# Attention by row pairs: bias rows added from their rows, K copied by ScalarE, the mask shared by two engines

## What is computed

```python
qkv = jnp.einsum('oc,bchw->bohw', qkv_w, x) + qkv_b[None, :, None, None]
q, k, v = (qkv[:, :C], qkv[:, C:2 * C], qkv[:, 2 * C:])
q = q * scale
k_u = unfold(k).reshape(B, nh, hd, L, ws * ws).transpose(0, 1, 3, 2, 4)
v_u = unfold(v).reshape(B, nh, hd, L, ws * ws).transpose(0, 1, 3, 4, 2)
k_g = k_u[:, :, attn_idx]
v_g = v_u[:, :, attn_idx]
attn = jnp.einsum('bnld,bnldk->bnlk', qh, k_g)
attn = attn + bias[None]
out = jnp.einsum('bnlk,bnlkd->bnld', attn, v_g)
```

## Time and profile before

| | us |
|---|---|
| median of 3 runs | 7908.27 (7907.89 to 7908.82) |
| profiled execution, its own time | 7900.45 |
| its span in the trace | 7898.5 |
| VectorE busy in the whole span | 6360.5 (81%) |
| TensorE, ScalarE, GpSimd busy | 6817.7 (86%), 5763.4 (73%), 5363.4 (68%) |
| row pairs of the first image, first to last add | 113.52 to 305.86 |
| row pairs of the second image, first to last add | 588.64 to 779.67 |

### The profile page before, as it was taken

One profiled execution on the slowest core, in us unless ns is written; L12 is line 12 of the kernel. 1 busy time (PEld: TensorE's weight loads), 2 busy tenths in 40 slices (PEclk: granted clock), 3 DMA queues, 4 the chain that ended last, 5 costly groups with the idle time before them and its releaser, 6 DMA issues. The chain is left out here.

```text
span 7898.5 us, 145982 instructions
## 1 busy us (share of the span) xinstructions
PE 6817.7 (86%) x42656; PEld 4640.5 (59%) x42656; DVE 6360.5 (81%) x9577; ACT 5763.4 (73%) x9016; POOL 5363.4 (68%) x3394
## 2 busy tenths in 40 slices
PE   5676787989968999999999999999999999999998
PEld 4444545767745666666666666665666666666666
DVE  3324184444439999999999999999999999999997
ACT  3416102222218999999999999999999999999997
POOL 3306000000009999999999999999999999999997
PEclk7878799999989999999999999999999999999998
DMA  1001000000010000000000000000000000000000
GB/s 65 22 3 38 0 0 0 0 0 0 0 58 10 1 1 1 1 1 1 10 1 1 1 1 1 1 27 1 1 1 1 1 2 2 3 3 3 4 4 5
DMA packets 75922, 55.73 MB, mean 7 GB/s; under 512 B 50776, under 2 KB 73464, under 8 KB 75032
## 3 DMA queue, kind: packets, MB, share of 16 engines
q1 hardware_dynamic: 72512, 53.88, 2.4%
q10 hardware_dynamic: 3288, 0.33, 0.0%
HBM read 37.80 MB, written 16.37 MB: 7 GB/s over the span
## 5 line engine op out<-in xcount | busy, mean ns | idle before, releaser
L1438 POOL TENSOR_TENSOR a_s<-a_s,a_v 128x784 f32<-128x784 f32 x1568 | 2910.3, 1856 | 429.5 <-ACT a_s L1650 414.0
L1474 PE MATMUL a_right_sides<-a_s,diag_d 128*128 128x392 f32 x6272 | 2281.7, 507 | 1.0 <-POOL a_s L1438 1.0
L1474 PEld LDWEIGHTS a_right_sides<-a_s,diag_d 128*128 128x128 f32 x6272 | 1130.6, 190 | 1035.9 <-issue 212.4
L1570 DVE SCALAR_TENSOR_TENSOR a_kan<-a_s,spline_c,a_kan 128x784 f32<-128x784 f32 x1568 | 1622.7, 1035 | 81.7
L1497 PEld LDWEIGHTS a_weighed<-a_V,a_probT 112*128 112x128 f32 x10976 | 1375.6, 193 | 162.2
L1431 POOL TENSOR_TENSOR a_inner<-a_inner,a_x 128x784 f32<-128x784 f32 x784 | 1456.8, 1858 | 0.0
L1497 PE MATMUL a_weighed<-a_V,a_probT 112*128 112x65 f32 x10976 | 1366.3, 270 | 0.0
L1650 ACT ACTIVATE a_s<-a_v 128x784 f32<-128x784 f32 x1568 | 1335.2, 852 | 4.6
L1641 ACT ACTIVATE a_v<-a_a 128x784 f32<-128x784 f32 x1568 | 1335.8, 852 | 0.3
L1486 PE MATMUL a_turned<-ident,a_prob 128*112 128x128 f32 x5488 | 856.7, 278 | 312.0 <-ACT a_probT L1657 305.7
L1461 PE MATMUL a_scores<-a_K,a_q 32*64 32x392 f32 x6272 | 699.6, 515 | 245.3 <-DVE a_kan L1552 214.6
(11 more groups left out here) (181 smaller groups left out, 6866.5 us busy)
## 6 DMA issues: line engine op xcount, KB each, us to landing
rows<-bias_rows_dram SPq DMA_DIRECT2D x112, 91.0 KB
X<-in_x_dram SPq DMA_DIRECT2D x4, 1568.0 KB, 15.8
a_q<-q_dram SPq DMA_DIRECT2D x392, 16.0 KB, 2.0
mask<-in_window_mask_dram SPq DMA_DIRECT2D x56, 98.0 KB
v_dram<-V SPq DMA_DIRECT2D x14, 227.5 KB, 2.3
a_V<-v_dram SPq DMA_DIRECT2D x4, 796.2 KB, 9.3
q_dram<-Q SPq DMA_DIRECT2D x14, 224.0 KB, 1.9
k_dram<-K SPq DMA_DIRECT2D x14, 224.0 KB, 1.9
```

The lines of the kernel that those rows point to most:

```text
L1438: eng.tensor_tensor(s, s, v, ALU.mult).then_inc(cubed, 1)
L1474: mm = eng.matmul(up[:, j, 0:SUB], steps[i][:, :], cubes[g][:, SUB * j:SUB * (j + 1)], start=(i == 0), stop=(i == 1))
L1570: eng.scalar_tensor_tensor(F, banked((s1, s2)[j][g][:, :]), c[:, 3 + j:4 + j], F, ALU.mult, ALU.add).then_inc(left_added, 1)
```

## The change

- The bias tile and ScalarE's copies into it are gone. VectorE adds the bias rows to the scores directly, with 8 instructions of 196 elements (L586 of the changed kernel) and 8 of 24 (L591); each reads one head of the rows, 8 floats apart, repeated over x.
- K's bias is added by ScalarE (L513), K and V have PSUM banks of their own (`kp[r]`, and `vp`, which exists once), and the scores wait for K's copy only; the weighing waits for V's.
- The mask is split: GpSimd multiplies 6 of the 8 blocks (L528), VectorE the other 2 (L597), right behind its add.
- SyncE loads the rows as soon as the add two tiles earlier is done, and the mask after both masks of two tiles earlier; the two kinds have semaphores of their own.
- The cleared margins are in `A` now, not in the bias tile.

```diff
             def _(sp):
                 def load(eng, t, r, turn):
-                    eng.wait_ge(masked, t + 1)
-                    eng.dma_start(mask[r][:, :], mask_dram[bass.ds(t, 1)].rearrange("t p c -> p (t c)")).then_inc(tables_loaded[r], 16)
-                    eng.wait_ge(bias_ready, t + 1)
+                    eng.wait_ge(scores_added, t + 1)
                     for q in range(2):
-                        eng.dma_start(rows[r][q * IMG:(q + 1) * IMG, :], bias_dram[bass.ds(2 * t + GRID * q, IMG), :]).then_inc(tables_loaded[r], 16)
+                        eng.dma_start(rows[r][q * IMG:(q + 1) * IMG, :], bias_dram[bass.ds(2 * t + GRID * q, IMG), :]).then_inc(rows_loaded[r], 16)
+                    eng.wait_ge(masked_p, t + 1)
+                    eng.wait_ge(masked_d, t + 1)
+                    eng.dma_start(mask[r][:, :], mask_dram[bass.ds(t, 1)].rearrange("t p c -> p (t c)")).then_inc(mask_loaded[r], 16)
...
             def _(act):
                 def stage(eng, t, r, turn):
-                    eng.wait_ge(kv_made, t + 1)
+                    eng.wait_ge(v_made, t + 1)
                     eng.activation(xt[r][:, :, :], xn[:, :, bass.ds(TILE * t, TILE)], ACT.Copy).then_inc(xt_ready, 1)
-                    eng.wait_ge(tables_loaded[r], 48 * (turn + 1))
+                    eng.wait_ge(k_made, t + 2)
                     eng.wait_ge(scores_added, t + 1)
...
                     for f in range(HALVES):
...
+                        eng.activation(kt[r][:, f, :], kp[r][:, f * TILE:(f + 1) * TILE], ACT.Identity, bias=m.qkvb[:, 2 + f:3 + f]).then_inc(kt_ready, 1)
+                act.sem_inc(kt_ready, 2 * HALVES)
                 ramp(act, stage, nothing)
...
                 def apply_mask(eng, t, r, turn):
-                    eng.wait_ge(tables_loaded[r], 48 * (turn + 1))
+                    eng.wait_ge(mask_loaded[r], 16 * (turn + 1))
                     eng.wait_ge(scores_added, t + 3)
-                    a = A[r][:, :, :, :].rearrange("p h f c -> p (h f) c")
-                    eng.tensor_tensor(a, a, mask[r][:, :].unsqueeze(1).to_broadcast([TILE, 8, COLS]), ALU.mult).then_inc(masked, 1)
...
+                    a = A[r][:, :, :, :].rearrange("p h f c -> p (h f) c")[:, 0:BY_POOL, :]
+                    eng.tensor_tensor(a, a, mask[r][:, :].unsqueeze(1).to_broadcast([TILE, BY_POOL, COLS]), ALU.mult).then_inc(masked_p, 1)
...
             def _(pe):
                 def front(eng, t, r, turn):
                     eng.wait_ge(xt_ready, t + 1)
-                    eng.wait_ge(kv_ready, 3 * (t + 1))
+                    eng.wait_ge(kt_ready, HALVES * (t + 1))
...
+                    mm.then_inc(k_made, 1)
+                    eng.wait_ge(vt_ready, t + 2)
                     for i in range(HALVES):
...
+                        mm = eng.matmul(vp[:, :], xt[r][:, i, :], m.WT[:, W_QKV + 8 + i:W_QKV + 12:2, :], start=(i == 0), stop=(i == HALVES - 1))
+                    mm.then_inc(v_made, 1)
+                    eng.wait_ge(kt_ready, HALVES * (t + 3))
                     eng.wait_ge(qt_ready, HALVES * (t + 1))
                     eng.wait_ge(scores_added, t + 2)
...
                 def back(eng, t, r, turn):
-                    eng.wait_ge(masked, t + 3)
+                    eng.wait_ge(vt_ready, t + 3)
+                    eng.wait_ge(masked_d, t + 3)
+                    eng.wait_ge(masked_p, t + 3)
                     eng.wait_ge(o_added, HALVES * (t + 1))
...
             def _(dve):
                 def front(eng, t, r, turn):
-                    eng.wait_ge(kv_made, t + 3)
+                    eng.wait_ge(v_made, t + 3)
+                    eng.tensor_tensor(vt[r][:, :], vp[:, :], m.vbias[0:TILE, :], ALU.add).then_inc(vt_ready, 1)
+                    eng.wait_ge(scores_made, t + 1)
+                    eng.wait_ge(rows_loaded[r], 32 * (turn + 1))
+                    window = rows[r][:, 0:WS * WIN * HEADS0].rearrange("p (y w e) -> p y w e", y=WS, w=WIN)
+                    beside = rows[r][:, WS * WIN * HEADS0:].rearrange("p (w s e) -> p w s e", w=WIN, e=HEADS0)
                     for f in range(HALVES):
-                        eng.tensor_scalar(kt[r][:, f, :], kvp[r][:, f * TILE:(f + 1) * TILE], m.qkvb[:, 2 + f:3 + f], None, ALU.add).then_inc(kv_ready, 1)
-                    eng.tensor_tensor(vt[r][:, :], kvp[r][0:TILE, 2 * TILE:2 * TILE + 2 * P], m.vbias[0:TILE, :], ALU.add).then_inc(kv_ready, 1)
-                    eng.wait_ge(scores_made, t + 1)
-                    eng.wait_ge(bias_ready, t + 3)
-                    eng.tensor_tensor(A[r][:, :, :, :].rearrange("p h f c -> p h (f c)"), scp[0:TILE, :, 0:HALVES * COLS],
-                                      bias[r][:, :, :, :].rearrange("p h f c -> p h (f c)"), ALU.add).then_inc(scores_added, 1)
+                        for h in range(4):
+                            cells = lambda ap: ap.rearrange("p (y x w) -> p y x w", y=WS, x=WS)
+                            eng.tensor_tensor(cells(A[r][:, h, f, 0:WS * WS * WIN]), cells(scp[0:TILE, h, f * COLS:f * COLS + WS * WS * WIN]),
+                                              window[:, :, :, 4 * f + h].unsqueeze(2).to_broadcast([TILE, WS, WS, WIN]), ALU.add)
+                    for f in range(HALVES):
+                        for h in range(4):
+                            cells = lambda ap: ap.rearrange("p (x w) -> p x w", w=WIN)[:, 1:WS, :]
+                            last = eng.tensor_tensor(cells(A[r][:, h, f, WS * WS * WIN:]), cells(scp[0:TILE, h, f * COLS + WS * WS * WIN:(f + 1) * COLS]),
+                                                     beside[:, :, :, 4 * f + h].rearrange("p w s -> p s w"), ALU.add)
+                    last.then_inc(scores_added, 1)
+                    eng.wait_ge(mask_loaded[r], 16 * (turn + 1))
+                    eng.wait_ge(scores_added, t + 3)
+                    a = A[r][:, :, :, :].rearrange("p h f c -> p (h f) c")[:, BY_POOL:8, :]
+                    eng.tensor_tensor(a, a, mask[r][:, :].unsqueeze(1).to_broadcast([TILE, 8 - BY_POOL, COLS]), ALU.mult).then_inc(masked_d, 1)
```

More of the change, by code:

```diff
@@ L456, in row_pairs0 @@
         mask = [sb(f"mask{r}", [TILE, COLS]) for r in range(2)]
-        bias = [sb(f"bias{r}", [TILE, 4, HALVES, COLS]) for r in range(2)]
         A = [sb(f"A{r}", [TILE, 4, HALVES, COLS]) for r in range(2)]
-        kvp = [ps(f"kvp{r}", [P, 512]) for r in range(2)]
+        kp = [ps(f"kp{r}", [P, 512]) for r in range(2)]
+        vp = ps("vp", [TILE, HALVES * P])
         scp = ps("scp", [P, 4, 512])
         op = ps("op", [P, 512])
[L464 to L467, removed]
+        xt_ready, qt_ready, k_made, v_made, kt_ready, vt_ready, margin_zeroed, scores_made, scores_added, o_made, o_added = (
+            sem(n) for n in ("xt_ready", "qt_ready", "k_made", "v_made", "kt_ready", "vt_ready", "margin_zeroed", "scores_made",
+                             "scores_added", "o_made", "o_added"))
+        masked_p, masked_d = sem("masked_p"), sem("masked_d")
+        rows_loaded = [sem(f"rows_loaded{r}") for r in range(2)]
+        mask_loaded = [sem(f"mask_loaded{r}") for r in range(2)]
+        BY_POOL = 6
         def ramp(eng, front, back):
@@ L558, in front @@
                         for h in range(4):
-                            rows = slice(HD0 * h, HD0 * (h + 1))
-                            mm = eng.matmul(scp[0:TILE, h, f * COLS:(f + 1) * COLS], kt[r][rows, f, :], qt[r][rows, f, :], start=True, stop=True)
+                            hd = slice(HD0 * h, HD0 * (h + 1))
+                            mm = eng.matmul(scp[0:TILE, h, f * COLS:(f + 1) * COLS], kt[r][hd, f, :], qt[r][hd, f, :], start=True, stop=True)
                     mm.then_inc(scores_made, 1)
                 def back(eng, t, r, turn):
-                    eng.wait_ge(masked, t + 3)
+                    eng.wait_ge(vt_ready, t + 3)
+                    eng.wait_ge(masked_d, t + 3)
+                    eng.wait_ge(masked_p, t + 3)
                     eng.wait_ge(o_added, HALVES * (t + 1))
@@ L593, in back @@
                         eng.tensor_tensor(dst, dst, fixed_cols(op[:, f * COLS:(f + 1) * COLS]), ALU.add).then_inc(o_added, 1)
-                dve.sem_inc(kv_ready, 6)
+                dve.sem_inc(vt_ready, 2)
                 dve.sem_inc(scores_added, 2)
+                dve.sem_inc(masked_d, 2)
                 dve.sem_inc(o_added, HALVES)
-                dve.sem_inc(bias_ready, 2)
+                dve.wait_ge(margin_zeroed, 2)
                 ramp(dve, front, back)
```

31 lines of the change are left out of this document (8 added, 23 removed).

## The result

The changed kernel takes 7995.47 us (median of 4 runs, 7985.16 to 8005.55), the kernel before 7908.08 in the same comparison. The ratio is 1.0113 with a 95% interval of 1.0095 to 1.013: 87 us slower, where 27 us faster was forecast and 7912 was the upper end of the range.

What follows compares the result with a forecast made beforehand. A loop of waits through GpSimd's mask, loads, ScalarE's bias copies and VectorE's add was taken to bound the row pairs at 7.10 us. Rounds 24.3 + heads 6.6 - tails 3.7 = 27 us saved, median 7881; range 7800 to 7912.

Steps and rivals of the forecast that it cites:

- The loop of the kernel before: Row pairs: mask, loads, ScalarE's bias copies and add take 14.26 us for two tiles; 8.1 us leave the path.
- The mask on VectorE: VectorE's round in the row pairs: masking 2 of 8 blocks, 448 elements, takes 0.62 us, 0.53 to the next start.
- Rival (d): Row pairs: VectorE's mask cannot run beside GpSimd's; round 9.4 us, 8029 us in all; chance 0.03.
- The strided add: VectorE's sixteen bias adds: two cycles per element read 32 bytes apart, 4.74 us, 4.83 with the tail.
- rival (b): VectorE's strided read costs ScalarE's 1.84 ns an element: add 4.5, round 6.35, 7864 us; chance 0.54 together with the forecast.
- 0.40 to 0.50: Sign on VectorE's large adds: the forecast is wrong if their starts are not this many us apart.
- TensorE's loop: Two-tile loop of mask, weighing, K, scores and add: 12.30 us at 2.4 GHz, 15.44 at 1.2 GHz.
- 12.30 / 2 = 6.15: TensorE's two-tile loop at 2.4 GHz gives 6.15 us a tile, just under VectorE's 6.36.
- Round: 1 / (0.75 / 6.36 + 0.25 / 7.72): Row-pair round with 25% of the time at 1.2 GHz: 6.65 us, against 7.10 before.
- K on ScalarE: ScalarE's two K bias copies take 0.7 us together; scores can start 2.2 us after K starts, before 3.20.
- GpSimd's price: GpSimd's mask in the row pairs: 2.12 ns an element and 0.2 fixed, so 1344 elements take 3.04 us.
- heads and tails: Ends of the two row-pair halves: earlier first adds save 6.6 us, longer tails lose 3.7.

Runs made afterwards that it cites:

- e2: Changed kernel with VectorE's mask issued as scalar_tensor_tensor instead of tensor_tensor; 7989.59 us, ratio 1.0078 to the kernel before.
- e3: Changed kernel with GpSimd's mask made to wait for VectorE's, so the two never overlap; 7916.54 us, ratio 0.9978 to the kernel before.
- e8: Changed kernel with VectorE's mask reading its sums from PSUM, next scores waiting for that mask; 7895.66 us, ratio 0.9985 to the kernel before.
- e4: Changed kernel with bias rows laid out by head, so VectorE's adds read adjacent floats; 7938.56 us, ratio 1.0008 to the kernel before.
- e10: e3 plus four matmuls of 128 x 256 that nobody reads behind every tile's scores; 7863.94 us, ratio 0.9942 to the kernel before.
- e6: e3 and e4 together: GpSimd's mask waits for VectorE's, bias rows by head; 7879.30 us, ratio 0.9964 to the kernel before.
- e9: e8 and e4 together: VectorE's mask reads from PSUM, bias rows by head; 7799.09 us, ratio 0.9863 to the kernel before.

## Why the prediction was wrong, point by point

**The loop of the kernel before.** Right as far as it was tested. Its waits for loads and bias copies are gone: in both halves together an add waits for a load once, 0.9 us at the head of the second half. What their going is worth by itself no run shows.

**The mask on VectorE: the step that failed.** "It gains the mask of 2 of 8 blocks ... 0.62" had the right work and the wrong company: the instruction took 3.48 us in 52 of 56 tiles, and no wait for GpSimd stood in the sum. Rival (d) described what happened, down to GpSimd's start 0.08 behind the add and VectorE's waiting for its end, and was given 0.03 because I read the earlier trace rows as two SBUF inputs. The row shows names, not memories; `a_kan` is allocated in PSUM, and the code before me said so. The row therefore said nothing about the case. No other row of the trace of before has VectorE reading two tensors of SBUF while GpSimd reads SBUF. So the trace was silent there, and the rule of the Trainium skill, SBUF — State Buffer, section Who interferes with whom, should have stood. It holds here in both directions: e2 shows the same with another kind of instruction, e3 that the time is waiting, e8 that one input in PSUM ends it. Rival (d)'s round of 9.4 used an add of 4.83; with the 4.16 measured it is 8.8, a little above the 8.59 of the timeline, since VectorE's mask needed 0.48 behind GpSimd's end and not the whole 0.62. Its 8029 us would be near 7995.

**The strided add.** Cheaper than the forecast and than rival (b): 0.484 us for 196 elements, of which 0.147 fixed leave 1.72 ns an element, where two cycles had been 2.08 and ScalarE's pace 1.84. The sixteen take 4.16 with the tail, not 4.83, and the large ones start 0.41 apart, just inside the 0.40 to 0.50 that was to show the forecast right. That the stride is the cause was argued then and is shown by e4.

**TensorE's loop and the clock: a second error, hidden by the first.** e3 keeps the two masks apart, and its round is 7.10, where the prediction's way of counting, with the add as measured and GpSimd's delay, gave 6.5. At the full clock that way of counting was right: 6.15 for e3's order, 6.15 measured in e10. The prediction's own 12.30 / 2 = 6.15 is the same number by luck: it counts 4.83 + 0.08 = 4.91 from the add's start to GpSimd's, all of it add and hand-over, and e10 takes 5.00, which are 4.2 of adds and then VectorE's mask. Wrong was the step "Round: 1 / (0.75 / 6.36 + 0.25 / 7.72)". It spreads the low clock evenly over the loop. But TensorE's clock is low behind its gap, and what stands behind the gap, weighing, K and V, is the part that lies on the path, while the gap itself passes at any clock. A shorter round gave no higher clock either: 0.84 in e3 and 0.75 in e6. e8, where the two masks run side by side, comes near the forecast of 6.65 with 6.82 and 6.66, and that is luck too. With the add at its measured price the same step would have said about 6.15 (an estimate: 5.82 from (12.30 - 0.67) / 2 and 7.39 from (15.44 - 0.67) / 2, in the same shares), so an add too dear and a low clock too cheap nearly cancel. Nor is e8 a clean measure, since its scores also wait for VectorE's mask.

**K on ScalarE, GpSimd's price.** Right: K's copies take 0.60 together (0.7 predicted), GpSimd's 1344 elements 3.02 (3.04 predicted). In e10 the scores start 1.94 us after K and not 2.2.

**The sign and the size.** 54 rounds of 8.46 - 7.10 make 73 us; row pairs as a whole lose 71, so heads and tails together gave back some 2, where 6.6 - 3.7 = 2.9 was forecast. The other 16 of the 87 stay open, as said above; the last layer alone varies by more from profile to profile.

## What to carry to other kernels

Before giving VectorE and GpSimd work at the same time, look up for each operand of the VectorE instruction whether it is in SBUF or in PSUM, in the allocation and not by its name: with two in SBUF, and GpSimd reading SBUF, the one that came second stood still here until the other had finished, and everything queued behind it waited too. Such a split gained here only with one of the inputs in PSUM (e8) or with the instructions kept apart in time (e3). And when a loop contains a gap of TensorE, price the matmuls right behind the gap at 1.2 GHz as well as at 2.4: a share of low clock spread over the loop misses where they stand.

## What the runs showed of the hardware that was not expected

- Filling a gap of 2.9 us with 2.0 us of useless matmuls made the round 0.95 us shorter (e3 to e10), since the granted clock went from 0.84 to 1.00. In e9, whose gaps are shorter, it is 1.00 without filling in the first half and 0.80 early in the second (550 to 570 us).
- VectorE pays 0.14 us for 196 floats of SBUF that lie 32 bytes apart and are repeated seven times (0.484 against 0.344 us); the repetition costs nothing. The same distance in PSUM cost nothing in the earlier trace rows.
- GpSimd's plain copy is stopped as well: two copies of the queries took 1.11 us where they met the end of VectorE's mask (changed kernel), 0.70 to 0.74 in the kernel before.
- Two instructions that are released by one semaphore reach their engines 0.02 to 0.05 us apart, and that decides which of them waits: 52 to 4 in the profile of the changed kernel.
